# First gated x made by GpSimd, and the first operations of VectorE and ScalarE in another order, in a mixture-of-experts kernel with adapter and layer norm

## The reference

```
g = h @ Wg[e];  u = h @ Wu[e]                       # D=128 -> F=512, for 8 experts
expert_output = sum over e of gate[b,e] * ((silu(g) * u) @ Wd[e])
shared = (silu(h @ Sg) * (h @ Su)) @ Sd
x = x + (1 - sg[b]) * expert_output + sg[b] * shared
h = relu(x @ W1[lang] + b1[lang]);  a = x + h @ W2[lang] + b2[lang]
x = x + ((a - mean(a)) * rsqrt(var(a) + 1e-5)) * gamma[lang] + beta[lang]
```

## Time and profile before

| | us |
|---|---|
| median of the three runs | 305.44 (305.38 to 305.45) |
| the profiled execution | 304.87 |
| span of its instructions | 303.1 |
| busy: TensorE / VectorE / ScalarE / GpSimd | 295.1 / 264.4 / 226.6 / 15.9 |

### The profile page before, as it was taken

One profiled execution on the slowest core, in us unless ns is written; L12 is line 12 of the kernel. 1 busy time (PEld: TensorE's weight loads), 2 busy tenths in 40 slices (PEclk: granted clock), 3 DMA queues, 4 the chain that ended last, 5 costly groups with the idle time before them and its releaser, 6 DMA issues.

```text
span 303.1 us, 4961 instructions
## 1 busy us (share of the span) xinstructions
PE 295.1 (97%) x1532; PEld 147.5 (49%) x1532; DVE 264.4 (87%) x590; ACT 226.6 (75%) x505; POOL 15.9 (5%) x24
## 2 busy tenths in 40 slices
PE   8999999999999999999999999999999999999983
PEld 3344444444444444444444444444444444688862
DVE  5999999998989898987779998699987899888894
ACT  5897878788878787877677776777777676688761
POOL 0200101200000000000010100101001010000000
PEclk9999999999999999999999999999999999999998
DMA  7990000014400000000000010000000000100000
GB/s 248 414 404 11 0 0 2 9 38 121 121 11 0 2 0 0 0 2 2 0 8 13 0 37 0 1 14 7 35 0 2 10 9 0 37 1 2 3 17 17
DMA packets 9133, 12.12 MB, mean 40 GB/s; under 512 B 3843, under 2 KB 6804, under 8 KB 9108
## 3 DMA queue, kind: packets, MB, share of 16 engines
q1 hardware_dynamic: 8962, 11.75, 11.3%
q10 hardware_dynamic: 146, 0.07, 0.1%
HBM read 10.76 MB, written 1.05 MB: 39 GB/s over the span
## 4 chain that ended last, share of the span: by engine, by line
PE 89%; issue 3%; DVE 1%; POOLq 0%; POOL 0%; DVEq 0%; ACT 0%
PE moe_ps L328 10%; PE moe_ps L330 10%; PE gate_ps L287 10%; PE moe_ps L327 10%; PE up_ps L309 10%; PE up_ps L312 10%; PE gate_ps L293 10%; PE gate_ps L290 10%; PE up_ps L306 10%; PE adapt_ps L353 1%; PE adapt_ps L340 1%; PE x_ps L345 1%; DVE hidden L500 0%; DVE h_lo L506 0%; DVE gx_lo L481 0%
## 5 line engine op out<-in xcount | busy, mean ns | idle before, releaser
L426 ACT ACTIVATE silu<-gate_ps 128x512 f32<-128x512 f32 (+1 forms) x160 | 88.6, 554 | 64.1 <-PE gate_ps L293 63.5
L500 DVE SCALAR_TENSOR_TENSOR hidden<-silu,up_ps 128x512 f32<-128x512 f32 (+1 forms) x160 | 100.7, 630 | 28.7 <-PE up_ps L312 22.6
L506 DVE TENSOR_TENSOR h_lo<-hidden,h_hi 128x512 f16<-128x512 f32 (+1 forms) x160 | 101.5, 635 | 0.1
L431 ACT ACTIVATE h_hi<-hidden 128x512 f16<-128x512 f32 (+1 forms) x160 | 92.8, 580 | 2.5 <-DVE hidden L500 2.2
L330 PE MATMUL moe_ps<-h_lo,w_hi 128*128 128x512 f16 (+1 forms) x160 | 57.3, 358 | 0.9 <-DVE h_lo L506 0.8
L309 PE MATMUL up_ps<-gx_lo,w_hi 128*128 128x512 f16 (+1 forms) x160 | 57.3, 358 | 0.7 <-DVE gx_lo L481 0.7
L287 PE MATMUL gate_ps<-x_hi,w_hi 128*128 128x512 f16 (+1 forms) x160 | 57.7, 360 | 0.0
L293 PE MATMUL gate_ps<-x_hi,w_lo 128*128 128x512 f16 (+1 forms) x160 | 57.5, 360 | 0.0
L290 PE MATMUL gate_ps<-x_lo,w_hi 128*128 128x512 f16 (+1 forms) x160 | 57.5, 360 | 0.0
L306 PE MATMUL up_ps<-gx_hi,w_hi 128*128 128x512 f16 (+1 forms) x160 | 57.3, 358 | 0.1
L327 PE MATMUL moe_ps<-h_hi,w_hi 128*128 128x512 f16 (+1 forms) x160 | 57.3, 358 | 0.0
(11 more groups left out here) (74 smaller groups left out, 146.4 us busy)
## 6 DMA issues: line engine op xcount, KB each, us to landing
w_full<-weights SPq DMA_DIRECT2D x8, 768.0 KB, 10.8
affine_sb<-affine SPq DMA_DIRECT2D x16, 128.0 KB, 2.9
x_full<-xT SPq DMA_DIRECT2D x4, 256.0 KB, 6.4
w_full<-weights SPq DMA_DIRECT2D x3, 256.0 KB, 4.3
out_dram<-result SPq DMA_DIRECT2D x3, 256.0 KB, 2.0
w2b_sb<-w2b SPq DMA_DIRECT2D x16, 16.5 KB
w_sb<-w SPq DMA_DIRECT2D x16, 16.0 KB
b_sb<-b SPq DMA_DIRECT2D x16, 0.1 KB
```

The costliest lines, as they stand in the source:

```text
L426: nc.scalar.activation(pair_slot(silu, n), gate_ps[n % 2][:, 0:STEPS[n][4]], ACT.Silu, scale=1.0 / W_SCALE).then_inc(silu_ready, 1)
L431: nc.scalar.activation(h_slot(h_hi, n), pair_slot(hidden, n), ACT.Copy).then_inc(h_hi_ready, 1)
L500: nc.vector.scalar_tensor_tensor(out=pair_slot(hidden, n), in0=pair_slot(silu, n), scalar=HIDDEN_RESCALE, in1=up_ps[n % 2][:, 0:STEPS[n][4 ...
L506: nc.vector.tensor_tensor(h_slot(h_lo, n), pair_slot(hidden, n), h_slot(h_hi, n), ALU.subtract).then_inc(h_lo_ready, 1)
```

## The change

The gates come in from memory as 128 equal rows instead of one (72 KB instead of 0.6), so the coefficient matmul, its ones and the copy out of PSUM are gone. GpSimd makes the coefficients, first those of expert 0 (16 columns), then the upper gated x of groups 0 and 1, eight pieces, each a multiplication by a column of `coef`; then `x_hi` of tile 1, then the coefficients of the shared expert and of experts 1 to 7 (`coef_ready`), and after up(0) `x_lo` of tile 1. ScalarE makes all three thirds of the first weights' upper half, and no piece of group 0 or 1; before `h_hi` of step 0 it waits for `coef_ready`. VectorE makes the lower halves only, and takes `hidden` of step 1 before `h_lo` of step 0 and before the last third of `w_lo`. TensorE has nine warm-up matmuls.

```diff
--- before.py
+++ after.py
@@ -16,8 +16,7 @@
 LANGS = 10
 LAG = 3
 LN_EPS = 1e-5
-WARM_UP = 8
-COEF_AT = 5
+WARM_UP = 9
 W_COLS = 3 * F
 GX_SLOTS = 4
...
@@ -78,13 +77,13 @@
     for i in range(BATCHES // 2):
         GX_AT.setdefault(len(WHOLE) + CHUNKS * (k - 1) + 2 * i, []).append(
             (len(GROUPS) - SPLIT + k % SPLIT, k // SPLIT * BATCHES // 2 + i))
-GX_AT[1] = [(1, 0), (1, 1)]
-GX_AT[2] = [(1, 2), (1, 3)]
+
+FIRST_GX = [(g, q) for g in (0, 1) for q in range(BATCHES)]
 
 W_AT = {2 * CHUNKS * e + s: (e + 1, third) for e in range(NE - 1)
         for third, s in enumerate((4, 5, 6) if e == 0 else (2, 4, 6))}
 
-X_AFTER = {1: 2, 2: 9, 3: 12}
+X_AFTER = {2: 9, 3: 12}
 
 
 def build(nc, xT, weights, gates, language, w1, w2b2, b1, affine, out):
...
@@ -277,12 +271,11 @@
                 t, e, f, at, width = STEPS[n]
                 hi, lo, psum = expert_w(w_hi, e, 0, f), expert_w(w_lo, e, 0, f), gate_ps[n % 2][:, 0:width]
                 x_at = slice(t * N + at, t * N + at + width)
-                if f == 0 and t == 0 and e > 0:
-                    pe.wait_ge(w_hi_ready, 3 * e)
+                if f == 0 and t == 0:
+                    pe.wait_ge(w_hi_ready, 3 * e + 1)
                 if n > 1:
                     pe.wait_ge(silu_ready, n - 1)
                 if n == 0:
-                    pe.wait_ge(w_first_hi_ready, 1)
                     pe.wait_ge(x_hi_ready, 1)
                 nc.tensor.matmul(psum, hi, x_hi[:, x_at], start=True, stop=False)
...
@@ -298,9 +291,12 @@
                 hi, lo, psum = expert_w(w_hi, e, 1, f), expert_w(w_lo, e, 1, f), up_ps[n % 2][:, 0:width]
                 gx_at = slice(g % GX_SLOTS * N + at, g % GX_SLOTS * N + at + width)
                 if f == 0 and t == 0:
-                    pe.wait_ge(w_hi_ready, 3 * e + 1)
+                    pe.wait_ge(w_hi_ready, 3 * e + 2)
                 if f == 0:
-                    pe.wait_ge(gx_hi_ready, gx_count[g, last_q])
+                    if g < 2:
+                        pe.wait_ge(gx_first_hi_ready, gx_count[g, last_q])
+                    else:
+                        pe.wait_ge(gx_hi_ready, gx_count[g, last_q] - len(FIRST_GX))
                 if n > 1:
                     pe.wait_ge(hidden_ready, n - 1)
                 nc.tensor.matmul(psum, hi, gx_hi[:, gx_at], start=True, stop=False)
...
@@ -355,13 +351,8 @@
                 last.then_inc(back_done, 1)
 
             pe.wait_ge(warm_ready, 1)
-            for i in range(WARM_UP):
+            for _ in range(WARM_UP):
                 nc.tensor.matmul(moe_ps[0][:, :], warm[:, 0:P], warm[:, :], start=True, stop=True)
-                if i == COEF_AT - 1:
-                    pe.wait_ge(ones_row_ready, 1)
-                    pe.wait_ge(coef_row_ready, 2)
-                    nc.tensor.matmul(coef_ps[:, 0:NE * B], ones_row[:, :], coef_row[:, :],
-                                     start=True, stop=True).then_inc(coef_spread, 1)
             gate(0)
             gate(1)
             for n in range(LAST + 1):
...
@@ -401,7 +392,7 @@
         @block.scalar
         def _(act):
             nc.scalar.preload_act_table(ACT.Silu)
-            act.dma_start(gates_row[:, :], gates).then_inc(gates_loaded, 16)
+            act.dma_start(gates_in[:, :], gates).then_inc(gates_loaded, 16)
 
             def gated_x_hi(g, q):
                 t, e = GROUPS[g]
...
@@ -446,14 +437,13 @@
 
             act.wait_ge(x_loaded[0], 16)
             nc.scalar.activation(cols(x_hi, 0, N), cols(x_full, 0, N), ACT.Copy).then_inc(x_hi_ready, 1)
-            act.wait_ge(coef_ready, 1)
-            for q in range(BATCHES):
-                gated_x_hi(0, q)
+            weight_hi(0, 0)
             weight_hi(0, 1)
             for n in range(LAST + 1):
                 silu_of(n)
-                if n == 0:
+                if n == 1:
                     weight_hi(0, 2)
+                    act.wait_ge(coef_ready, 1)
                 if n > 0:
                     hidden_hi(n - 1)
                 for g, q in GX_AT.get(n, ()):
...
@@ -477,17 +467,17 @@
             def gated_x_lo(g, q):
                 t, e = GROUPS[g]
                 batch = t * BATCHES + q
-                dve.wait_ge(gx_hi_ready, gx_count[g, q])
+                if g < 2:
+                    dve.wait_ge(gx_first_hi_ready, gx_count[g, q])
+                else:
+                    dve.wait_ge(gx_hi_ready, gx_count[g, q] - len(FIRST_GX))
                 nc.vector.scalar_tensor_tensor(out=gx_part(gx_lo, g, q), in0=cols(x_full, batch, S),
                                                scalar=coef[:, e * B + batch:e * B + batch + 1],
                                                in1=gx_part(gx_hi, g, q), op0=ALU.mult,
                                                op1=ALU.subtract).then_inc(gx_lo_ready, 1)
 
             def weight_lo(e, third):
-                if e == 0 and third == 0:
-                    dve.wait_ge(w_first_hi_ready, 1)
-                else:
-                    dve.wait_ge(w_hi_ready, 3 * e + third)
+                dve.wait_ge(w_hi_ready, 3 * e + third + 1)
                 nc.vector.scalar_tensor_tensor(out=cols(w_lo, 3 * e + third, F), in0=cols(w_full, 3 * e + third, F),
                                                scalar=W_SCALE, in1=cols(w_hi, 3 * e + third, F), op0=ALU.mult,
                                                op1=ALU.subtract).then_inc(w_lo_ready, 1)
...
@@ -568,40 +558,27 @@
                         norm_out(j, i)
 
             nc.vector.memset(warm[:, :], 0.0).then_inc(warm_ready, 1)
-            nc.vector.memset(ones_row[:, :], 1.0).then_inc(ones_row_ready, 1)
-            dve.wait_ge(gates_loaded, 16)
-            shared_in = gates_row[:, B * (NE - 1):]
-            nc.vector.tensor_scalar(rest_row[:, :], shared_in, -X_SCALE, X_SCALE, ALU.mult,
-                                    ALU.add).then_inc(rest_ready, 1)
-            nc.vector.tensor_scalar(coef_row[:, (NE - 1) * B:], shared_in, X_SCALE, None,
-                                    ALU.mult).then_inc(coef_row_ready, 1)
-            dve.wait_ge(rest_ready, 1)
-            nc.vector.tensor_tensor(coef_row[:, 0:(NE - 1) * B].rearrange("p (e b) -> p e b", b=B),
-                                    gates_row[:, 0:B * (NE - 1)].rearrange("p (b e) -> p e b", b=B),
-                                    rest_row[:, :].rearrange("p (o b) -> p o b", o=1).to_broadcast([1, NE - 1, B]),
-                                    ALU.mult).then_inc(coef_row_ready, 1)
-            dve.wait_ge(coef_spread, 1)
-            nc.vector.tensor_copy(coef[:, :], coef_ps[:, 0:NE * B]).then_inc(coef_ready, 1)
-            dve.wait_ge(w0_loaded[0], 16)
-            nc.vector.tensor_scalar(cols(w_hi, 0, F), cols(w_full, 0, F), W_SCALE, None,
-                                    ALU.mult).then_inc(w_first_hi_ready, 1)
             dve.wait_ge(x_hi_ready, 1)
             nc.vector.tensor_tensor(cols(x_lo, 0, N), cols(x_full, 0, N), cols(x_hi, 0, N),
                                     ALU.subtract).then_inc(x_lo_ready, 1)
             weight_lo(0, 0)
-            dve.wait_ge(coef_ready, 1)
             for q in range(BATCHES):
                 gated_x_lo(0, q)
             weight_lo(0, 1)
+            for q in range(BATCHES // 2):
+                gated_x_lo(1, q)
             for n in range(LAST + 1):
                 hidden_of(n)
                 for j, (_, _, _, at) in enumerate(JOBS):
                     if n == at:
                         moe_out(j)
-                if n == 0:
-                    weight_lo(0, 2)
+                if n == 1:
+                    for q in range(BATCHES // 2, BATCHES):
+                        gated_x_lo(1, q)
                 if n > 0:
                     hidden_lo(n - 1)
+                if n == 1:
+                    weight_lo(0, 2)
                 for g, q in GX_AT.get(n, ()):
                     gated_x_lo(g, q)
                 if n in W_AT:
...
@@ -635,13 +612,44 @@
 
         @block.gpsimd
         def _(pool):
-            for t in range(1, TILES):
-                pool.wait_ge(x_loaded[t], 16)
-                pool.wait_ge(w_lo_ready, X_AFTER[t])
+            def first_gx_hi(g):
+                for q in range(BATCHES):
+                    nc.gpsimd.tensor_scalar(gx_part(gx_hi, g, q), cols(x_full, g * BATCHES + q, S),
+                                            coef[:, g * BATCHES + q:g * BATCHES + q + 1], None,
+                                            ALU.mult).then_inc(gx_first_hi_ready, 1)
+
+            def x_upper(t):
                 nc.gpsimd.tensor_copy(cols(x_hi, t, N), cols(x_full, t, N)).then_inc(x_rest_hi_ready, 1)
+
+            def x_lower(t):
                 pool.wait_ge(x_rest_hi_ready, t)
                 nc.gpsimd.tensor_tensor(cols(x_lo, t, N), cols(x_full, t, N), cols(x_hi, t, N),
                                         ALU.subtract).then_inc(x_rest_ready, 1)
+
+
+            pool.wait_ge(gates_loaded, 16)
```

(25 more changed lines are left out.)

15 lines of the change are left out of this document (5 added, 10 removed).

## The result

| | before | after |
|---|---|---|
| median, us | 305.29 (304.87 to 305.45, 6 runs) | 306.36 (306.25 to 306.57, 6 runs) |
| profiled execution / its span | 304.87 / 303.1 | 306.57 / 304.8 |
| busy: TensorE / VectorE / ScalarE / GpSimd | 295.1 / 264.4 / 226.6 / 15.9 | 294.5 / 264.1 / 224.7 / 22.6 |
| first down matmul starts | 11.67 | 14.14 |
| step 4's second up matmul starts (the mark) | 13.86 | 15.66 |

A forecast was written before the change was run, and what follows sets the result against it. VectorE's queue and data arrival were taken to bound the first 14 us. A first down matmul at 12.22 against 12.35 gave -0.13 us on 305.44, so 305.3 us, forecast as no change (53%); range 304.6 to 306.4.

The forecast's parts named there:

- The decisive place and its chain: First down matmul: coefficients at 9.51, then x_lo's port turn, gx_lo, h_lo and last w_lo, start at 12.22.
- rival D: GpSimd's first operation: pool configuration delays the first coefficients, down matmul at 12.95, at least +0.6, 306.1 us; 3%.
- Rival C: Shared port: each GpSimd record holds VectorE for its full length; down matmul at 13.2, +0.85, 306.3 us; 8%.
- the price of a piece: GpSimd's 128-wide gated x multiplications: 0.25 us each, taken from a select on 128x128 with a record of 0.29.
- at 0.6 about +1.6: Bound for GpSimd's pieces: at 0.6 us each, counted four times after x's landing, the sum is about +1.6 us.
- -0.13: First down matmul: forecast start 12.22 minus 12.35, the start of an equally fast undisturbed run, in us.
- the landings' ends of 0 and 0.5: Bounds on the delay of transfers by the wider gates: 0 gives a sum of -0.2, 0.5 gives +0.1 us.
- rival B: GpSimd's pieces: fixed 0.35 or more per operation with an SBUF coefficient, piece 0.45; +0.8, 306.2 us; 15%.
- 0.2 for every landing: Input transfers: the 72 KB of gates delay each landing by 0.2 us, out of an estimated 0.2 to 0.5.
- TensorE at 7.32 with the first up matmul: Front of TensorE: first up matmul starts at 7.32, 0.18 us earlier than before, if the faster rate comes at the same moment.
- what would make the prediction wrong: TensorE waiting for gx_hi or w_lo at the first up matmul, or a new wait after 14 us.
- Clock: none: Bounds: the clock was given no effect on the forecast sum.

The follow-up runs named there:

- e10: Changed kernel with each tile's four GpSimd multiplications made one of 512 columns by the number 4.0; 305.32 us (one run).
- e3b: Changed kernel with the gates' transfer issued by SyncE ahead of x of tile 0 instead of by ScalarE; 306.20 us, ratio 1.0046.
- e4b: Changed kernel with tile 1's four upper pieces back on ScalarE, VectorE's lower ones behind them, tile 0's still on GpSimd; 305.31 us.
- e9: Kernel before with 128-row gates, coefficients on VectorE, nine warm-ups, and the last third of w_lo after the second hidden; 304.10 us, ratio 0.9967.
- e14: e9 with the one-row float32 matmul put back among eight warm-ups, its result unread; 305.00 us, ratio 0.9996.
- e5: Changed kernel with all eight upper pieces on ScalarE and tile 1's lower ones behind them; 304.39 us, ratio 0.9975.
- e13: Changed kernel with real pieces on ScalarE, four unread pieces on GpSimd, ScalarE's wait for all coefficients moved to step 3; 305.02 us.

## Why the prediction was wrong

**What held.** The decisive place and its chain: coefficients complete, `h_hi` and x_lo's turn, `h_lo`, the last third of `w_lo`, the first down matmul; from coefficients to matmul 2.31 us against 2.71 forecast (the difference is mostly the piece of `gx_lo`, which no longer stood in between). One large wait there, none behind it. The pool-configuration instruction takes 11 ns and delays nothing: rival D is out. Rival C, the lock for the whole record, is out as well: `h_lo` from 12.53 beside x_lo from 11.79 to 12.94 takes 0.96. If its own work is 0.68, it began at 12.81, 0.13 before the end of x_lo's record, as in the earlier trace rows. C's time, 306.3, agrees with the measured one, but by this row not for C's reason. The Trainium skill ("SBUF — State Buffer", "Who interferes with whom") has the second wait until the first finishes; the turns agree, the length is again shorter than the record.

**The step that failed: the price of a piece.** "I take 0.25 per piece" was wrong: it is 0.58 from start to start. The row that I took it from, a select of 128 columns in 0.29, was of another kind of operation, and by e10 0.25 happens to be the part of the price that doesn't depend on the columns. It counted eight times and not four: tile 0's pieces were still running when x of tile 1 landed at 7.03. From the forecast 9.51 to the measured 11.83 for the coefficients: tile 1's first piece started at 7.67 instead of 6.87 (0.80, of it 0.20 the landing); its four took 2.69 instead of 1.39 to the cast (1.30); cast and coefficients 1.47 instead of 1.25 (0.22). That is 2.32; less 0.40 gained behind them it is 1.92, the distance from 12.22 to 14.14. The bound "at 0.6 about +1.6" is near the 1.80 of the mark, but in part by luck: by its own rule, four pieces at 0.35 more each on -0.13, it is +1.3 (and the landings' ends of 0 and 0.5 give -0.3 and +0.2, not -0.2 and +0.1). The missing part is that the price counts eight times. What happened is rival B, *dear pieces*, at a price above the one that it was given; its mechanism, a fixed cost of an operand from SBUF, is not what the runs show.

**The smaller one: the landings.** I had the gates at 2.5 and 0.2 for every landing. Gates came at 4.09, x of tile 0 0.6 later, x of tile 1 0.4 later. With the gates' part taken back, e3b regains 0.53 of the 1.80.

**What I left out.** Beside the sum, the forecast had TensorE at 7.32 with the first up matmul. It came at 7.83, after 0.68 of idle time for GpSimd's fourth piece: I had named this as what would make the prediction wrong. It was covered by the later wait, so it costs nothing in after; in e4b, where the first down matmul waits for nothing, it counts. And the rest of the change, the layout with VectorE's order, is worth 1.0 us of the medians (e9), a gain that the change holds and the pieces spend. 0.56 of it shows at the mark and is the order's; the other part comes from fewer long executions. "Clock: none" may have hidden that part, since the layout also frees the warm-ups of the one-row matmul; e14 supports it and doesn't settle it.

## What to carry to other kernels

Before work moves to GpSimd, find a row of the same kind of operation at the same width; where there is none, take the dear end as the forecast if the count is high, since an error of 0.33 us in the price of one, eight times in a row, is more than the whole loss here. Ask of every GpSimd operation which VectorE operation it will fall beside: next to one that reads PSUM x_lo was free (two `hidden` took 1.33 beside it in e5), next to one with two inputs in SBUF it cost its turn (`h_lo` 1.55 in e13). And even an operation whose result is never read can push a later one to such a place. And take a mixed change apart before giving it up: here two of its parts, without the third, are worth 0.33%.

## What was not expected of the hardware

GpSimd's multiplication of float32 by one scalar per partition to float16 grows by 0.0026 us per column on 0.25 fixed, so that 512 columns take 1.56 from start to start (a record of 1.49), while the record of a cast of the same 512 is 0.60 and that of the product of two inputs 1.04. The Trainium skill ("GPSIMD Engine Reference", section "Engine selection") calls its one-input operations "roughly line-rate" beside VectorE; the cast comes nearer to this, 0.60 for 512 columns where VectorE's multiplication of the same width, `w_hi`, takes 0.42; GpSimd's multiplication, with 1.49, does not. A transfer of 128 rows of 576 B landed 3.3 after its issue beside the 256-KB load of x, and 1.9 after it when it was first in the queue. And with a one-row matmul among the warm-ups the matmuls became fast at 7.04, 7.07 and 8.87 in the three profiled executions that have it, against 4.08 (e4b) to 7.03 (e13) without it.
